# Two-layer residual kernel: layer 1 as three products of 256 columns into one PSUM region

## The reference

```python
# layer 0: a linear layer plus a signed mask product, scaled per batch
sign = 2 * mask - 1                                    # mask: (8, 1024, 1024) int32
x = x + x @ W0.T + b0 + coeff[b] * (x @ sign[b])
# layer 1: a linear layer plus a low-rank adapter of rank 16, chosen per batch
h = x @ lora_A[ids[b]].T                               # (256, 16)
x = x + x @ W1.T + b1 + h @ lora_B[ids[b]].T
```

## Time and profile before

| | |
|---|---|
| median of 3 runs | 438.1 us (437.32 to 438.97) |
| the profiled execution | 438.86 us, of which 437.1 us span from first to last instruction |
| mean granted TensorE clock over the span | 0.992 of full |
| PE, DVE, ACT, POOL busy | 405.9, 286.0, 235.9, 14.0 us |

### The profile page before, as it was taken

One profiled execution on the slowest core, in us unless ns is written; L12 is line 12 of the kernel. 1 busy time (PEld: TensorE's weight loads), 2 busy tenths in 40 slices (PEclk: granted clock), 3 DMA queues, 4 the chain that ended last, 5 costly groups with the idle time before them and its releaser, 6 DMA issues.

```text
span 437.1 us, 5483 instructions
## 1 busy us (share of the span) xinstructions
PE 405.9 (93%) x2033; PEld 339.5 (78%) x2033; DVE 286.0 (65%) x334; ACT 235.9 (54%) x350; POOL 14.0 (3%) x26
## 2 busy tenths in 40 slices
PE   0586999788999999999999999999999999999996
PEld 0474888566888888888888888888888888888884
DVE  1717656787678765886588767876588658865512
ACT  1727667546445755656556644575565555665412
POOL 1212020000000000000000000000000000000000
PEclk9996999999999999999999999999999999999999
DMA  8698399345963299237922595329823692254002
GB/s 197 194 314 258 91 248 241 96 86 162 212 144 97 76 226 197 66 97 177 232 77 83 162 221 134 96 80 232 189 66 97 155 250 81 82 162 114 1 0 97
DMA packets 92542, 63.29 MB, mean 145 GB/s; under 512 B 3547, under 2 KB 86499, under 8 KB 92516
## 3 DMA queue, kind: packets, MB, share of 16 engines
q1 hardware_dynamic: 92516, 62.95, 57.2%
HBM read 51.39 MB, written 8.39 MB: 137 GB/s over the span
## 4 chain that ended last, share of the span: by engine, by line
PE 85%; SPq 4%; DVE 4%; ACT 2%; DMA 2%; issue 2%; ACTq 0%
PE ps L591 25%; PE ps L618 13%; PE ps L617 13%; PE ps L593 13%; PE ps L619 13%; PE ps L601 3%; PE ps L577 3%; DMA wm<-in_mask_Bx4096x_ik_dram 2%; PE ps L629 2%; SPq L234 1%; SPq L190 1%; DVE wlo L473 1%; SPq L192 1%; ACT w1hi L325 1%; DVE wm L467 1%
## 5 line engine op out<-in xcount | busy, mean ns | idle before, releaser
L591 PE MATMUL ps<-xhl,whi 128*128 128x512 f32 x512 | 187.6, 405 | 4.3 <-DVE wlo L473 3.5
L593 PE MATMUL ps<-xhl,wlo 128*128 128x256 f32 x512 | 144.9, 283 | 0.0
L591 PEld LDWEIGHTS ps<-xhl,whi 128*128 128x128 f32 x512 | 97.6, 191 | 27.1 <-DVE wlo L473 3.6
L473 DVE TENSOR_TENSOR wlo<-wm,whi 128x1024 fp32r<-128x1024 f32 x64 | 78.4, 1225 | 48.7 <-ACT whi L337 48.7
L337 ACT ACTIVATE whi<-wm 128x1024 fp32r<-128x1024 f32 x64 | 67.8, 1059 | 73.9 <-DVE wm L467 72.7
L617 PE MATMUL ps<-w1hi,yhl 128*128 128x512 f32 x256 | 101.8, 398 | 0.0
L618 PE MATMUL ps<-w1lo,yhl 128*128 128x512 f32 x256 | 100.7, 393 | 0.0
L619 PE MATMUL ps<-w1hi,yhl 128*128 128x512 f32 x256 | 100.5, 393 | 0.0
L593 PEld LDWEIGHTS ps<-xhl,wlo 128*128 128x128 f32 x512 | 98.1, 192 | 2.4
L467 DVE SCALAR_TENSOR_TENSOR wm<-wm,cs,w0t 128x1024 f32<-128x1024 f32 x64 | 81.4, 1273 | 14.1 <-ACT w0t L315 14.1
L330 ACT ACTIVATE wm<-wm 128x1024 f32<-128x1024 int32 x64 | 67.4, 1054 | 8.2 <-DMA wm<-in_mask_Bx4096x_ik_dram 8.2
(11 more groups left out here) (42 smaller groups left out, 168.0 us busy)
## 6 DMA issues: line engine op xcount, KB each, us to landing
wm<-in_mask_Bx4096x_ik_dram SPq DMA_DIRECT2D x64, 512.0 KB, 4.4
xraw<-in_x_dram SPq DMA_DIRECT2D x32, 256.0 KB, 7.1
out_dram<-zst SPq DMA_DIRECT2D x32, 256.0 KB, 2.5
w0raw<-in_L_cond_W_dram SPq DMA_DIRECT2D x8, 512.0 KB, 7.1
w1raw<-_L_cond_base_weight_dram SPq DMA_DIRECT2D x8, 512.0 KB, 6.5
bt<-bhl SPq DMA_DIRECT2D x48, 64.0 KB, 2.9
abraw<-in_L_cond_lora_A_w_dram SPq DMA_DIRECT2D x8, 64.0 KB, 2.6
abraw<-in_L_cond_lora_B_w_dram SPq DMA_DIRECT2D x8, 64.0 KB, 1.8
```

The source lines that it names most:

```text
L473: nc.vector.tensor_tensor(wlo[:, s, :, :], wm[:, n % MS, :].rearrange("p (k o) -> p k o", k=KT), whi[:, s, :, :].bitcast(F32), ALU.subtrac ...
L591: nc.tensor.matmul(ps[:, bank, :], whi[:, s, k, :], xhl[:, b % 2, k, :], start=(k == 0), stop=False, skip_group_check=True)
L593: op = nc.tensor.matmul(ps[:, bank, 0:S], wlo[:, s, k, :], xhl[:, b % 2, k, 0:S], start=False, stop=(k == KT - 1), skip_group_check=True)
```

## The change

Layer 1 makes its three products one after the other, each of 256 columns, all into columns 0 to 255 of the bank. y is then complete in PSUM but for the bias. ACT takes the high part straight from PSUM with the bias added; DVE takes PSUM plus bias minus the high part in one scalar_tensor_tensor. `half_y`, `make_y`, the tile `ysum` and the semaphores `y_half` and `y_made` are gone. Where `half_y` stood, `y_parts_hi` stands now, ahead of the splits of W1 and of `sign`; in batch 0 `y_parts_lo` stands where `make_y` stood. PE waits for `y_lo` in place of `y_made`.

```diff
-            def half_y(n):
+            def y_parts_hi(n):
                 act.wait_ge(l1_done, n + 1)
                 if n == 0:
                     act.wait_ge(b0_moved, 1)
                 if n >= 2:
-                    act.wait_ge(y_lo, n - 1)
-                nc.scalar.activation(ysum[:, n % 2, :], ps[:, L1B + n % 2, S:2 * S], ACT.Identity,
-                                     bias=b0col[:, n % KT:n % KT + 1]).then_inc(y_half, 1)
-
-            def y_parts_hi(n):
-                act.wait_ge(y_made, n + 1)
-                if n >= 2:
                     act.wait_ge(l2_done, n - 1)
-                nc.scalar.activation(yhl[:, n % 2, 0:S], ysum[:, n % 2, :], ACT.Copy).then_inc(y_hi, 1)
+                nc.scalar.activation(yhl[:, n % 2, 0:S], ps[:, L1B + n % 2, 0:S], ACT.Identity,
+                                     bias=b0col[:, n % KT:n % KT + 1]).then_inc(y_hi, 1)
...
-            def make_y(n):
-                dve.wait_ge(y_half, n + 1)
-                row = ysum[:, n % 2, :]
-                nc.vector.tensor_tensor(row, ps[:, L1B + n % 2, 0:S], row, ALU.add).then_inc(y_made, 1)
-
             def y_parts_lo(n):
                 dve.wait_ge(y_hi, n + 1)
-                nc.vector.tensor_tensor(yhl[:, n % 2, S:2 * S], ysum[:, n % 2, :], yhl[:, n % 2, 0:S].bitcast(F32),
-                                        ALU.subtract).then_inc(y_lo, 1)
+                nc.vector.scalar_tensor_tensor(yhl[:, n % 2, S:2 * S], ps[:, L1B + n % 2, 0:S],
+                                               b0col[:, n % KT:n % KT + 1], yhl[:, n % 2, 0:S].bitcast(F32),
+                                               ALU.add, ALU.subtract).then_inc(y_lo, 1)
...
                     if n >= 2:
-                        pe.wait_ge(y_made, n - 1)
+                        pe.wait_ge(y_lo, n - 1)
                 for k in ks:
...
-                    nc.tensor.matmul(ps[:, bank, :], whi[:, s, k, :], xhl[:, b % 2, k, :],
-                                     start=(k == 0), stop=False, skip_group_check=True)
+                    nc.tensor.matmul(ps[:, bank, 0:S], whi[:, s, k, :], xhl[:, b % 2, k, 0:S],
+                                     start=(k == 0), stop=False)
+                    nc.tensor.matmul(ps[:, bank, 0:S], whi[:, s, k, :], xhl[:, b % 2, k, S:2 * S],
+                                     start=False, stop=False)
                     op = nc.tensor.matmul(ps[:, bank, 0:S], wlo[:, s, k, :], xhl[:, b % 2, k, 0:S],
-                                          start=False, stop=(k == KT - 1), skip_group_check=True)
+                                          start=False, stop=(k == KT - 1))
```

More of the change, by code:

```diff
@@ L73, in two_layer_kernel @@
         xt2 = nc.alloc_sbuf_tensor_at("xt2", [P, TG, S], F32, offset=yhl_at)
-        ysum_at = nc.sbuf_base
-        ysum = sb("ysum", [P, 2, S])
-        b0row = nc.alloc_sbuf_tensor_at("b0row", [KT, P], F32, offset=ysum_at)
+        b0row = sb("b0row", [KT, P])
         zst_at = nc.sbuf_base
@@ L129, in two_layer_kernel @@
         l1_done = sem("l1_done")
-        y_half = sem("y_half")
-        y_made = sem("y_made")
         y_hi = sem("y_hi")
@@ L403, in _ @@
                     split_hi("b", 0, 1)
-                half_y(n)
+                y_parts_hi(n)
                 if n == 0:
@@ L412, in _ @@
                 split_hi("w1", n, 1)
-                y_parts_hi(n)
                 if n == 1:
@@ L513, in _ @@
                     split_lo("b", 0, 1)
-                make_y(n)
+                y_parts_lo(n)
                 if n == 0:
@@ L519, in _ @@
                 split_lo("w1", n, 1)
-                y_parts_lo(n)
                 if n in (5, 7):
```

## The result

The changed kernel takes 439.41 us (median of 20 runs, 437.92 to 440.44) against 438.22 us (20 runs) of the kernel before: ratio 1.0027, 95% interval 1.0015 to 1.0038. It is about 1.2 us slower, where 2.6 us less was forecast. Ratios and their intervals go over all undisturbed executions of both kernels, and can differ a little from the quotient of two medians.

What follows compares the result with a forecast made beforehand. The prediction took PE's instruction stream to bound the kernel, with ACT and DVE mattering only in batch 0. From 438.86 us, -1.6 -1.0 gave 436.3, and 0.8 less for the median gave 435.5; range 430 to 441.

Steps and rivals of the forecast that it cites:

- Part 1: PE, layer 1: three 256-column products per k instead of one long and one short; -1.0 us, bounds -5.7 to +4.6.
- part 4: Batch 0's path: ACT and DVE instructions removed ahead of things PE waits for; -1.6 us, bounds -0.8 and -2.2.
- nearest row: Layer 1's existing short product, read as 116.4 ns; three take 349.3 ns against 351 per k, -1.0 us.
- rival 2: PE: a fixed price per product, 4.3 ns per cut, 512 cuts +2.2 us, time 438.7; chance 0.18.
- The two ends: Bounds for layer 1's short product: half of layer 2's 226.7 ns, -5.7 us; half of 0.24 us, 120 ns, +4.6 us.
- Rival 1: Layer 1's even stream settles at half of 226.7 ns per product: -5.7 us, time 430.8; chance 0.22.
- Rival 3: PE's weight load becomes the bound under short products; at 120 ns a step the time is 441.1; chance 0.15.
- Rival 4: PE's instruction supply becomes the bound: +0.6 us per chunk, +35 in all, about 470; chance 0.03.
- Part 2: ACT loses 64 instructions of 414 ns, the remaining one takes 469 ns; 26.5 us freed, priced nothing in batches 1 to 7.
- part 3: DVE loses 64 additions of 421 ns; new form taken as 440 ns, upper bound 473; about 26 us freed, off the path.
- The four waits: PE's batch 0 waits for `bhl`, `ht`, `w1lo` and `xhl`, 5.9 us in sum, forecast to fall to about 4.5.
- this sign of being wrong: PE's half-rate clock stretch at 35.5 us moves or vanishes, worth up to 2 us either way.

Runs made afterwards that it cites:

- products_alone: Kernel before with layer 1's 512-column product cut into two of 256, old destinations and old y chain kept: 441.16 us against 437.73, ratio 1.0072.
- three_products_grouped: Changed kernel with, per group of k, the high-weight products first and then all low-weight ones: ratio 1.0040 to the kernel before.
- long_then_short: Kernel before with, per group of k, all 512-column products of layer 1 first, then all 256-column ones: 435.56 us against 437.73, ratio 0.9932.
- 64/128: Changed kernel with layer 1's products in one batch loading 64 columns and streaming 128; only the step was read: 60 ns a product.
- y_chain_alone: Changed kernel's y chain with layer 1's products as before, one term left out of y: 437.11 us against 437.73, ratio 0.9983.

## Why the prediction was wrong

**Part 1 is the step that failed**, in the price of the short product. It took the short product's line, 15.9% of 328 us, and divided it by 448 products: 116.4 ns, three of them 349.3 against 351, and so -1.0 us. The window holds 440 of them, so that the row says 118.5 ns. Three times that is 355.6, over 512 k +2.2 us in place of -1.0, and already above the 118.1 at which the prediction itself let part 1 eat up part 4. Counted rightly, its own nearest row would have put the time at 438.7, still 0.7 below the one measured.

What the runs showed in its place: in the changed kernel, in products_alone and in three_products_grouped a short product among its like costs 120 ns, so k costs 359 (2.87 us over eight), 7.5 ns more than before. Of the 3.6 ns between 116.4 and 120, 2.1 are the count; the other 1.5 are that beside a long product the short one is a little cheaper and the long one dearer, 233.3 ns against the 226.7 that it takes among its like, in layer 2 or in long_then_short. With what layer 2 gives back, the term is +2.2 us in the seven later batches (2.6 if batch 0 loses as much per chunk), in place of -1.0.

**The mechanism was rival 2's**, a price for each cut, and its +2.2 us and its 438.7 came close, but by luck. Its 4.3 ns per cut came from the miscounted 116.4 and from layer 2's average of 228.5. Among equal products a cut costs 13.3 ns: 2 x 120 against 226.7. In layer 1 the cut also ended the alternation, which had cost 6 ns per k (351 against 345), and layer 2 gave some back. In a stream of equal products with 128 columns loaded, one of at least 256 columns costs N/2.4 + 13.3 ns within 2 ns: the steps are 120, 132, 147, 175 and 227 at 256, 288, 320, 384 and 512 columns. The two ends that I had in hand were right by themselves, 226.7 for a long one in an even stream and 120 as the upper end for a short one. The Trainium skill's "Back-to-back issue gap" in "TensorE: Matmul & The Clock Gate" gives an isolated matmul the same form with 2.5 ns; the slope agrees with the trace, the constant does not, for this kernel's float32r products with a load each.

**Rival 1 fell**: the even stream settled at once, but at 120 and not at half of a long one. **Rival 3** named the right step, 120 ns, for a reason that the runs bear out only in part. The load of 128 columns alone has its floor at 108 to 111 ns (64 to 224 columns streamed), so it is not what bounds the step at 256. But it has a share in the 120, since with 64 or 80 columns loaded the step is 114. **Rival 4 fell**: 64/128 ran a load and a product in 60 ns, over eight k.

**Part 2 and part 3** held in kind. The new DVE form was dearer than my upper end, 481 ns against 473, and the new ACT form takes 473 where 469 was assumed. That explains only part of why ACT is 21.8 us less busy and DVE 19.4, and not 26 each. The rest, some 4 us on either engine, is that I added up durations while neighbours overlap: the durations of all groups sum to about 15.6 us more than ACT's busy time before and 11 after, and on DVE to 12 before and 8 after. Part 4 says itself that the step between starts counts; parts 2 and 3 did not use it. Both lie off the path of the later batches, and cost nothing.

**Part 4** was right in its list and too large in its sum. The four waits fell by 1.5 us in the changed kernel (forecast 1.4) and by 1.2 in y_chain_alone. What I left out is what comes late next: W1's slices arrive by DMA, and PE waited 0.8 to 0.9 us for one, at 65 us in the changed kernel and at 74 in y_chain_alone. Before, POOL was done with the first of these at 63.07 and PE began on it at 65.08, and with the second at 72.3 and 72.87. Why the first comes later in the kernels with three products no run tells. In time the y chain gave 0.7 us, between 0 and 1.6. The half-rate stretch of PE came 1.5 us earlier (33.95 to 40.78 after 35.50 to 42.32) and was as long as before, 6.83 us. PE was busy for 4.58 us of it in place of 5.04, so by estimate 0.2 us less was spent there at half pace; this sign of being wrong did not decide.

**The sum, with what was measured.** The 1.12 us by which batch 0 finished earlier in the profiled execution are less than the 1.6 of part 4, and not all of them are the change's: PE's first product, a transpose that no changed instruction precedes, began 0.50 us earlier (10.55 after 11.05), and it begins at 11.34 in y_chain_alone and at 10.32 in products_alone, as W0 arrives. If that lead carried through, 0.6 us is left for the change in batch 0, near the 0.7 above. The seven later batches lost 2.20, and 0.2 were lost outside the span, which the sum had left at 1.8. The two parts run alone, 3.2 and -0.7, add up to 2.5 against the 1.2 measured (0.7 to 1.7); with intervals of 1.1 and 0.8 on either side that is no contradiction.

The reserve named at the end, that short products might not keep 116 to 117 ns in a row, is what happened; they did not have 116.4 before either.

## What to carry to other kernels

Where a share of a window is divided by a count, take the count from the trace of that window: here one chunk of 56 decided the sign. Take the price of a matmul from a run of its like: in an alternating pair one member may be paying for the other. Cutting a product of 512 columns in two costs PE 13 ns here among equal products, and 7.5 where the cut ends an alternation, so on a PE-bound kernel an operation saved on ACT or DVE has to stand on PE's path to pay for it. Before changing the work, try its order: all long products and then all short ones gave 0.7% with nothing else changed, more than the change studied here was forecast to bring.

## What the runs showed of the hardware that was not expected

- Alternating 512- and 256-column products cost 351 ns a pair, separated 345 (346.7 by the price above); with long ones first, a batch grouped in twos or eights is 0.5 us shorter, in fours 0.24. No run tells why.
- At 320 and 384 columns streamed a product takes 147 and 173 to 175 ns whether 64 or 128 columns are loaded. At 256 the step is 120 with 128 loaded, 114 with 80 or 64, and again 117 and 118 with 48 and 32; at 512 it is 226.7 with 128 and 230 with 64. No run tells why either.
- In products_alone PE waited 1.9 us for `bhl` up to 80.65, as in the kernel before (1.9 up to 80.86), but this time the granted clock fell to 1.2 GHz from 81.84 to 85.25, after which it was full again:

```profile
81.84:85.25 3.41, 3.41 (x12) 2.50 (x11) 1.42 (x2) 1.30 (x3) 0.00 (x0) 0.50 0.31 95
```

  At half pace that stretch holds 1.7 us less work, in that one execution. Yet the `finish` of batch 0 began only 0.17 us later than in the kernel before (102.96 after 102.79), with PE's first product 0.73 us sooner. So under 1 us of it was left by then; the second wait for `bhl`, 0.8 us in the kernel before, is gone from this trace.
